# Start-up transfers gathered in one queue, first scores in the tiles' banks, later zero fills moved, and new step orders in a two-layer MoE kernel

## What is computed

```
x = x + 0.5 * L0_ffn(layernorm(x))      # 8 experts, argmax routing, gelu, no capacity limit
x = x + L0_attn(layernorm(x))           # conv, q/k/v with running sums, gelu MLP of width 512
x = x + 0.5 * L0_ffn(layernorm(x))      # the same 8 experts again
x = x + 0.5 * L1_ffn(layernorm(x))      # 16 experts, capacity 320, relu, weighted by the softmax
x = x + L1_attn(layernorm(x))           # u @ W_b, a linear recurrence, @ W_c, layernorm
x = x + 0.5 * L1_ffn(layernorm(x))      # the same 16 experts again
```

## Time and profile before

| | |
|---|---|
| runs | 761.2, 763.09, 762.07 us, median 762.07 |
| the profiled execution | 764.19 us, its span 762.9 us |
| granted TensorE clock, mean | 0.895 of full speed |
| busy in the span | PE 608.2, PEld 494.3, DVE 432.9, ACT 332.7, POOL 387.9 us |
| DMA | 95.39 MB, mean 125 GB/s |
| chain that ended last, by engine | PE 55%, DVE 11%, POOL 10%, issue 10%, DMA 5%, ACT 2% |

### The profile page before, as it was taken

One profiled execution on the slowest core, in us unless ns is written; L12 is line 12 of the kernel. 1 busy time (PEld: TensorE's weight loads), 2 busy tenths in 40 slices (PEclk: granted clock), 3 DMA queues, 4 the chain that ended last, 5 costly groups with the idle time before them and its releaser, 6 DMA issues.

```text
span 762.9 us, 13462 instructions
## 1 busy us (share of the span) xinstructions
PE 608.2 (80%) x3640; PEld 494.3 (65%) x3640; DVE 432.9 (57%) x1670; ACT 332.7 (44%) x989; POOL 387.9 (51%) x386
## 2 busy tenths in 40 slices
...
GB/s 329 245 148 331 159 246 208 257 218 84 1 0 1 1 85 43 93 78 189 166 177 213 89 124 114 81 127 139 148 114 130 36 82 56 79 91 128 139 42 13
DMA packets 75257, 95.39 MB, mean 125 GB/s; under 512 B 12658, under 2 KB 51481, under 8 KB 74928
## 3 DMA queue, kind: packets, MB, share of 16 engines
...
## 4 chain that ended last, share of the span: by engine, by line
PE 55%; DVE 11%; POOL 10%; issue 10%; DMA 5%; ACT 2%; SPq 1%; DVEq 0%; ACTq 0%; POOLq 0%
PE ps L689 10%; PE ps L696 9%; PE ps L624 8%; PE ps L616 8%; POOL xs L1260 6%; PE ps L671 3%; PE ps L664 3%; PE ps L575 2%; PE ps L539 2%; PE ps L638 2%; PE ps L679 2%; DMA xs<-X,IDX 2%; POOL sma L1257 1%; PE ps L703 1%; POOL X L1275 1%
## 5 line engine op out<-in xcount | busy, mean ns | idle before, releaser
L1260 POOL DMA_INDIRECT xs<-X,IDX x128 | 127.2, 994 | 65.2 <-issue 48.0
L1169 ACT ACTIVATE ht<-ps,CL 128x128 f32<-128x128 f32 x368 | 103.6, 375 | 96.5 <-PE ps L616 93.6
L1264 POOL DMA_INDIRECT y<-yt,xi x92 | 90.4, 983 | 88.0 <-DVE yt L942 70.8
L616 PE MATMUL ps<-xt,w1s 128*128 128x128 f32 x736 | 103.4, 289 | 14.1 <-DMA w1s<-in_w 7.0
L616 PEld LDWEIGHTS ps<-xt,w1s 128*128 128x128 f32 x736 | 95.1, 203 | 17.7 <-DMA w1s<-in_w 8.2
L624 PE MATMUL ps<-W,ht 128*128 x736 | 102.4, 287 | 3.9 <-ACT ht L1169 2.9
L624 PEld LDWEIGHTS ps<-W,ht 128*128 128x128 f32 x736 | 93.0, 200 | 8.0 <-issue 7.7
L1257 POOL TENSOR_TENSOR sma<-sma,MH 128x4 f32<-128x4 f32 (+1 forms) x40 | 48.4, 1212 | 75.1 <-DVE sma L734 59.6
L1226 ACT ACTIVATE hb<-ps 128x320 f32<-128x320 f32 x64 | 27.9, 436 | 83.5 <-PE ps L689 83.5
L1264 POOL DMA_INDIRECT y<-xu,x x36 | 34.4, 954 | 45.6 <-DVE xu L1050 35.3
L1038 DVE TENSOR_SCALAR hb<-ps 128x320 f32<-128x320 f32 x64 | 31.4, 491 | 37.6 <-PE ps L689 36.9
...
## 6 DMA issues: line engine op xcount, KB each, us to landing
...
```

Of the source, the lines that this page charges most:

```text
L616: r = e.matmul(ps[TILE_BANKS[i % n]][:, c * P:(c + 1) * P], W1[i % NW1][:, c * P:(c + 1) * P], XTT[i % NX][:, :], start=True, stop=True)
L1169: r = e.activation(HT[i % NHT][:, c, :], ps[TILE_BANKS[i % len(TILE_BANKS)]][:, c * P:(c + 1) * P], ACT.Gelu, bias=CL[:, bass.ds(r0 * 4 + ...
L1260: return e.indirect_dma_start(dst, bass.IndirectOffsetOnAxis(ap=IDX[:, n:n + 1], axis=0), X[:, n, :], None, bounds_check=hi, oob_is_err=False)
L1264: return e.indirect_dma_start(dst, bass.IndirectOffsetOnAxis(ap=ix, axis=0), src, None, bounds_check=NT * P - 1, oob_is_err=False)
```

## The change

The zero fills of later groups and four large start-up transfers move, the scores of the first block get other banks, one wait is added for `pturn`, and all five step strings are new. The diff, with the strings cut to two lines:

```diff
-FILL_AFTER = [8, 12] + [18 + 3 * k for k in range(8)]
+FILL_AFTER = [("aout", n) for n in (1, 2, 3, 3, 4, 4)] + [("edown", n) for n in (2, 4, 6, 8)]
 
 TABLE = {
     "sp": """
...
-tload.83 tw.74 tw.75 tload.84 tw.76 tw.77 tload.85 tw.78 tload.86 yload.8 tw.79 yload.9 yload.10 yload.11 yload.12 tw.80 tload.87 tload.88 tw.81
...
+yload.7 fill.0 fill.1 fill.2 fill.3 fill.4 fill.5 tw.46 tw.47 tw.48 tw.49 tload.46 tload.47 tload.48 tload.49 tload.50 tload.51 tload.52 tload.53
...
@@ ring_of
-    if stage == "pscore" and i != BATCH[BOF[i]][0]:
+    if stage == "pscore" and (i < NC or i != BATCH[BOF[i]][0]):
         return None
@@ bank
-            return ps[PLACE[stage, i][0]]
+            return ps[TILE_BANKS[BOF[i]] if stage == "pscore" and i < NC else PLACE[stage, i][0]]
@@ sp_program
             for c in range(TURNED + 1, NC):
                 load_x(c)
 
+            e.dma_start(KC[:, K_E:K_END], consts[:, K_E:K_END]).then_inc(sem("ce"), 16)
+            e.dma_start(W02[:, :], w02).then_inc(sem("cw"), 16)
+            e.dma_start(RW[:, V_B2:V_END], rows[V_B2:V_END].partition_broadcast(P)).then_inc(sem("cw"), 16)
+            e.dma_start(CL[:, :], cols).then_inc(sem("cw"), 16)
+
             for stage, i in ORDER["sp"]:
                 if stage == "fill":
-                    SP.wait_ge(sem("tturn"), FILL_AFTER[i + 2])
-                    fill1(e, i // 4, i % 4)
+                    name, n = FILL_AFTER[i]
+                    SP.wait_ge(sem(name), n)
+                    if i < 2:
+                        fill0(e, i + 2)
+                    else:
+                        fill1(e, (i - 2) // 4, (i - 2) % 4)
@@ pe_program
                     PE.wait_ge(sem("ck"), 16)
+                    if i:
+
+                        PE.wait_ge(sem("ra"), 1)
                     wait_x(PE, k)
...
-                    b = (take("pscore", i) if i == k0 else bank("pscore", k0))[:, (i - k0) * CT * en:(i - k0 + 1) * CT * en]
+                    b = (take("pscore", i) if i == k0 >= NC else bank("pscore", k0))[:, (i - k0) * CT * en:(i - k0 + 1) * CT * en]
...
                     if i >= n:
                         PE.wait_ge(sem("ty"), i - n + 1)
+                    else:
+                        PE.wait_ge(sem("plog"), 2 * i + 1)
@@ act_program
                 if stage == "bulk":
-
-                    ACTE.wait_ge(sem("cenc"), 1)
                     if i == 0:
-                        e.dma_start(KC[:, K_E:K_END], consts[:, K_E:K_END]).then_inc(sem("ce"), 16)
-                        e.dma_start(W02[:, :], w02).then_inc(sem("cw"), 16)
-                    elif i == 1:
-                        e.dma_start(RW[:, V_B2:V_END], rows[V_B2:V_END].partition_broadcast(P)).then_inc(sem("cw"), 16)
-                        e.dma_start(CL[:, :], cols).then_inc(sem("cw"), 16)
-                    elif i == 2:
                         ACTE.wait_ge(sem("rsel"), 2)
                         fill0(e, 1)
-                    elif i == 3:
+                    else:
                         ACTE.wait_ge(sem("rsel"), 4)
                         e.dma_start(RW[:, E0:V_B2], rows[E0:V_B2].partition_broadcast(P)).then_inc(sem("cb"), 16)
                         e.dma_start(MT[:, :], mats).then_inc(sem("cm"), 16)
-                    else:
-                        ACTE.wait_ge(sem("tturn"), FILL_AFTER[i - 4])
-                        fill0(e, i - 2)
```

More of the change, by code:

```diff
@@ L71 @@
[L71 to L74, removed]
@@ L79 @@
[L79 to L82, removed]
@@ L88 @@
[L88 to L91, removed]
@@ L96 @@
[L96 to L99, removed]
@@ L100 @@
[L100 to L103, removed]
@@ L108 @@
[L108 to L111, removed]
@@ L137 @@
-apoolq.4 ax2.3 apoolk.4 amulv.4 astat3.3 ax2.4 astat3.4 anorm3.3 astat1.7 anorm3.4 axb.4 anorm1.6 axb2.1 axb2.2 axb2.3 anorm1.7 aout.1 pstat.9 aout.2
-pstat.10 axb2.4 axb.5 peps.3 axb.6 pnm.3 acb.5 aout.3 axb.7 acb.6 acb.7 pstat.11 aout.4 pstat.12 peps.4 pnm.4 plog.3 oh.3 plog.4 oh.4 ra.2 ax1.5 rb.2
-astat2.5 rte.2 rsel.2 anorm2.5 ax1.6 astat2.6 ax1.7 astat2.7 apoolq.5 apoolk.5 anorm2.6 amulv.5 anorm2.7 ax2.5 axb2.5 astat3.5 anorm3.5 apoolq.6
-apoolq.7 apoolk.6 amulv.6 apoolk.7 amulv.7 ax2.6 astat3.6 ax2.7 astat3.7 anorm3.6 txb.46 tn.46 txb.47 anorm3.7 tn.47 axb2.6 aout.5 axb2.7 tx.46
@@ L141 @@
-pstat.13 tx.47 tn.48 txb.48 txb.49 tn.49 tn.50 tx.48 tn.51 ty.46 txb.50 tx.49 tn.52 ty.47 txb.51 ty.48 txb.52 tx.50 tn.53 aout.6 pstat.14 peps.5 aout.7
-ty.49 txb.53 pnm.5 pstat.15 tx.51 peps.6 tn.54 pnm.6 ty.50 txb.54 plog.5 tx.52 oh.5 tx.53 tn.55 plog.6 oh.6 ra.3 tx.54 ty.51 txb.55 ty.52 txb.56 tn.56
-tx.55 rb.3 tx.56 rte.3 ty.53 txb.57 tn.57 ty.54 txb.58 tn.58 tx.57 tn.59 ty.55 tx.58 txb.59 tn.60 tn.61 tx.59 rsel.3 tx.60 ty.56 txb.60 ty.57 tx.61
-txb.61 tn.62 tn.63 tn.64 tx.62 tn.65 tx.63 ty.58 txb.62 ty.59 txb.63 tn.66 tn.67 tx.64 ty.60 tx.65 txb.64 tn.68 ty.61 txb.65 ty.62 txb.66 tx.66 tn.69
@@ new lines @@
+pstat.0 pstat.1 peps.0 pstat.2 pnm.0 plog.0 oh.0 ra.0 pstat.3 rb.0 rte.0 rsel.0 pstat.4 pstat.5 pstat.6 pstat.7 peps.1 peps.2 pnm.1 plog.1 oh.1 plog.2
+pnm.2 oh.2 ra.1 rb.1 rte.1 rsel.1 tn.0 tn.1 tx.0 tn.2 tn.3 tx.1 tn.4 txb.0 txb.1 txb.2 txb.3 tx.2 tn.5 wc.0 tx.3 tn.6 ty.0 txb.4 tx.4 ty.1 txb.5 ty.2
+txb.6 tn.7 tx.5 tn.8 ty.3 txb.7 tx.6 tn.9 ty.4 txb.8 tx.7 tn.10 ty.5 txb.9 tx.8 tn.11 ty.6 txb.10 tn.12 tx.9 ty.7 txb.11 tn.13 tx.10 ty.8 txb.12 tn.14
+tx.11 ty.9 txb.13 tx.12 tn.15 ty.10 txb.14 tx.13 tn.16 ty.11 txb.15 tx.14 ty.12 txb.16 tn.17 tx.15 ty.13 txb.17 tn.18 tx.16 tn.19 ty.14 txb.18 tx.17
@@ new lines @@
+apoolq.4 anorm3.3 apoolk.4 pstat.8 axb2.1 aout.1 pstat.9 amulv.4 acb.5 ax2.4 astat3.4 axb2.2 astat1.7 anorm3.4 anorm1.6 axb.3 axb2.3 anorm1.7 axb.4
+aout.2 axb2.4 pstat.10 peps.3 axb.5 axb.6 pnm.3 aout.3 pstat.11 acb.6 acb.7 axb.7 aout.4 pstat.12 peps.4 plog.3 pnm.4 oh.3 plog.4 oh.4 ra.2 ax1.5 rb.2
+astat2.5 rte.2 rsel.2 anorm2.5 ax1.6 astat2.6 ax1.7 astat2.7 anorm2.6 apoolq.5 apoolk.5 anorm2.7 amulv.5 apoolq.6 ax2.5 astat3.5 apoolk.6 anorm3.5
+amulv.6 apoolq.7 ax2.6 astat3.6 apoolk.7 amulv.7 anorm3.6 axb2.5 axb2.6 ax2.7 astat3.7 axb2.7 anorm3.7 aout.5 txb.46 txb.47 txb.48 txb.49 pstat.13
```

214 lines of the change are left out of this document (119 added, 95 removed).

## The result

The changed kernel takes **737.95 us** (median of 4 runs, 737.15 to 739.93) beside 762.58 us for the kernel before on the same chip: ratio 0.968, 95% interval 0.966 to 0.971, so 24.6 us faster. The forecast was 743, its range 731 to 757. The profiled execution of the changed kernel took 738.26 us, its span 737.0.

What follows compares the result with a forecast made beforehand. Bound by a chain of waits: routing, POOL's sends, late tile weights; 16-expert stages already full on PE. Terms -8.3 - 1.9 - 6.7 + 1.8 + 1.2 - 5 = -18.9, against the median 762.07 giving 743 us, range 731 to 757.

Steps and rivals of the forecast that it cites:

- Start, -8.3: Up to group 1's first send: chunk 3's rows and the routing come sooner, send at 41.3 for 49.58 us, -8.3.
- Landing, -1.9: Group 1's last send: lands in nearer 2.28 than 4.23 us without fills beside it, -1.9, bounds 0 and -2.
- Tiles of group 1, -6.7 and +1.8: Group 1's tiles: weight waits and a slow tile go with the fills, -6.7; one more tile behind the restart, +1.8.
- My own sign for a wrong account: Group 1's tiles: the account is wrong if they take over 80 us from their restart.
- Moved fills, 0: Attention and first experts: the fills moved there cost 0; without cover some 2 us per step of four, at most 8.
- Group 2: Group 2's sends: the power `apow3.6` stands between them and costs +1.2 us.
- The attention's own order, "even": Attention before group 2: its new order taken as neither gain nor loss, bounds -4 and +3 us.
- Group 3, -5: Group 3: sends 60 to 63 no longer behind homes, sends over by 371 us; -5, bounds 0 and -9.6.
- The stop of 4.66 and a slow down-product, 2.07 for 1.06, can go: PE before group 3: sooner sends remove the stop until 387.32 us and the slow product behind it, 5.7 us.
- late next: POOL from 354.5 to 475.3 us: transfers and powers fill 111 of 121 us, leaving little room beyond group 3's -5.
- more than I count: Rival, 731 us: the attention's -4, the rest of POOL's -4.6 and -2 to -3 of small gaps also come; chance 0.09.
- The rival on one queue: Start: one queue brings the rows no sooner, -4.4 for -8.3, time 747 us; chance 0.06.

Runs made afterwards that it cites:

- b_both: Kernel before with the four start transfers moved to SP's queue and the zero fills moved, orders as before: ratio 0.984, median 752.64 us.
- b_queue: Kernel before with only the four start transfers moved from ACT's queue to SP's, behind the eight chunks: ratio 0.995, median 761.17 us.
- b_fills: Kernel before with only the zero fills moved, into the attention and beside the first experts: ratio 0.990, median 756.48 us.
- after: The changed kernel itself, with all of the change, against the kernel before: 737.95 us, ratio 0.968.
- a_fills_back2: Changed kernel with the zero fills put back amid the tiles of group 1, on the slower kind of chip: ratio to the kernel before 0.982, median 784.75 us.
- h_newhead: Changed kernel with new orders up to the first tile of group 2, old orders behind; slower kind of chip: ratio to the kernel before 0.979.
- h_oldhead: Changed kernel with old orders up to the first tile of group 2, new orders behind; slower kind of chip: ratio to the kernel before 0.983.
- a_queue_back: Changed kernel with the four start transfers back on ACT's queue: ratio to the kernel before 0.973, median 743.2 us.
- after_again: The changed kernel run once more, unaltered, on the slower kind of chip: ratio to the kernel before 0.969.

## Why the prediction was right, and where not

**Start, -8.3: -9.8.** Mechanism as put. The three turns took 2.80 us, not 3 x 1.1, and `rbase.0` came at 19.5 for 20.4. Queue 4.5, order 5.2.

**Landing, -1.9: -1.9**, by b_both and b_queue the fills' doing. PE's start gained 1.1 us less than the landing: from landing to PE 3.77 us passed where it had been 2.65. The first rows were there 2.5 us after their issue, not 1.8, and `txb`, which now stands ahead of `tx.13` on DVE, makes it 1.25 us from the rows to PE where it had been 0.80.

**Tiles of group 1, -6.7 and +1.8: -3.0 in all.** The -6.7 was well sized: b_fills has -7.2. The term that was mis-sized is the other, the price of the new order, +1.8: the new order takes 80.1 us, +4.2 against the 75.9 of b_fills and +2.9 against the 77.2 of b_both, which has the sooner start too. The one more tile behind the restart costs its 1.9 as priced. The rest I had put at nothing: I had not looked at where the attention's moments stand on DVE, with their wait for rows that go to DRAM and back, and that wait stopped PE for 2.5 us. b_both and after are level at the last down-product (155.6, 155.4), although the latter's sends start 4.0 us sooner: by then the new order has given all that back. My own sign for a wrong account, over 80 us from the restart, is just met.

**Moved fills, 0:** right, by b_fills, as far as the attention goes. Alone the move is worth 7.4 us; with the new order, by `a_fills_back2` and on the other kind of chip, about 10.

**Group 2.** `apow3.6` +1.2: the sends took 30.1 us for 28.7, +1.4. **The attention's own order, "even": -3.1** (101.7 us for 104.7; 105.1 to 106.2 in b_queue, b_fills and b_both). Which of its moves gives it was not looked into.

**Group 3, -5: -9.6, for another reason.** The step "The stop of 4.66 and a slow down-product, 2.07 for 1.06, can go" put the gain on POOL's order. The stop is gone (from 305 to 385 us PE waits nowhere longer than 1.1 us), but from the first send of group 3 to the last of the 16-expert block it is only 2.1 us. The last down-product of group 3 ends 3.8 us sooner in that stretch, but POOL, named as late next, has its last twelve sends one behind the other before and now. The other 7.5 come before, where I had counted nothing: 2.3 by the ranking, since the attention of chunk 7 is done sooner behind the sends of group 2, and 6.0 behind it, since PE no longer does seven tile products ahead of `rbase`, less 0.7 for a home. I had read POOL and PE only from 354.5 on. The pair h_newhead and h_oldhead, on the slower kind of chip, bears this out: each has one of the two and not the gain.

**Rest.** Another 1.0 us behind the last send. The terms as measured: -9.8 - 0.8 - 3.0 - 3.1 + 1.4 - 7.5 - 2.1 - 1.0 = -25.9. Forecast -18.9. The time lies between the forecast and the rival "more than I count" (731), 5 us below the one. The attention did come near its bound of -4. That group 3 stands at its bound of -9.6 is chance: the bound was worked out for POOL's transfers, and the gain came from PE's and DVE's order.

The rival on one queue was refuted: 5.2 us at the first send in b_queue, 4.5 in a_queue_back. The reason may be in the earlier trace rows themselves, which I had not read so far: the two queues moved nearly as many packets, 46 and 48, and one's were almost eight times as large. The Trainium skill states just this ("DMA: Bandwidth & Descriptors", section "Queues, rings and completion order": an engine takes turns between queues packet by packet); the near-equal counts of the trace agree, though no run changed the size of the packets. The section of the Trainium skill that I weighed instead says that transfers interleave, and nothing of who is served first.

## What to carry to other kernels

If a small-packet transfer is urgent, keep large-packet transfers out of the other queues until it is through; one queue in order of need did it here. A gain at the start is worth its whole size only if nothing behind it is late by itself: by the spans the queue alone kept 1.9 of 5.2 us, beside the moved fills 3.2 of 6.1, and in the changed kernel 4.3 of 4.5. For each group's routing ask which chunk comes last, what stands ahead of it on PE and DVE, and what stands between one step of the routing and the next: seven tile products ahead of one small matmul cost 6.0 us here. And a step whose input goes to DRAM and back should stand behind the work that does not need it.

## What the chips showed

On two chips the kernel before took 810 us, and it and the changed kernel some 47 us more than on the others. In after_again, PE in order of time:

```profile
69.93 2.04 PE L631 MATMUL ps<-xt,w1s 128*128 128x128 f32 x8 [15.06 <-issue]
```

ACT stood from 51.1 to 74.8, DVE from 53.2 to 69.5, while POOL sent on. DMA queues from 53 to 70 us, first in after_again, then in after:

```profile
q0 software_dynamic: 416, 0.88, 15.4%
q1 hardware_dynamic: 288, 0.33, 6.4%
```

```profile
q14 instruction: 3, 0.02, 0.5%
q8 instruction: 1, 0.02, 0.4%
```

The two instruction queues moved nothing there on the slower chip (4 packets on the other), and the same number, 3 and 1, from 70 to 90, when group 1's sends were over:

```profile
q14 instruction: 3, 0.02, 0.4%
q8 instruction: 1, 0.02, 0.3%
```

It is tempting to say that the engines waited for these packets, but the order of time speaks against it: the first of them moved at 76.6 us, when DVE (69.5), PE (69.9) and ACT (74.8) were at work again. They may be missing because the engines stood still. SP was slow before it stopped, too: its register step ahead of a weight load took 0.70 us at 52.6 where it takes 0.05. What held the engines is open; what the trace shows is that it began during group 1's sends and ended with them or within some us (the last begins at 68.5). Another 21 us are lost between the last send of group 3 and the last of the 16-expert block (123.1 us for 102.3). Why it happens on some chips and not on others, and whether fewer or later sends would avoid it, was not tried.
